# Two attentions in one kernel: maxima turned by one transpose a group, last values beside the spread, Q, K and V biases on ScalarE, the causal diagonal masked on VectorE behind the exponential

## The chip, the cores and the metric

The kernel runs on one core of a Trainium2 chip. The metric is the device time of one execution in microseconds (us). The engines are TensorE (PE in the rows, its weight loads PEld), VectorE (DVE), ScalarE (ACT), GpSimd (POOL) and SyncE (SP), which issues most DMAs.

## The reference

A layer of a gated cross-attention model on x of shape 8 x 512 x 512 (batch, tokens, channels), all in float32, cut to what matters:

```python
# pass A: cross attention, 16 heads of 32
Q = (layernorm(x) @ Wq + bq), K = (ctx @ Wk + bk), V = (ctx @ Wv + bv)   # split in heads
scores = Q @ K.T / sqrt(32) + rel_bias[:, clip(i - j, -63, 63) + 63]; masked keys -> -inf
x = x + tanh(g_xattn) * (softmax(scores) @ V @ Wo + bo)
# pass B: causal self attention with a latent K/V and rotary parts, 16 heads of 64
h = rmsnorm(layernorm(x), w_ln1)
q = h @ Wq, kv = (h @ Wkva)[..., :64] @ Wkvb, k_rope = (h @ Wkva)[..., 64:]
q = [q_nope, rope(q_rope)], k = [kv, rope(k_rope)], v = [kv, 0]
att = q @ k.T / sqrt(64); att = where(lower triangle, att, -inf)
y = layernorm(x) + softmax(att) @ v @ Wo
# pass C: router over 8 experts, top 2, and a shared expert; out = x + tanh(g_ffn) * (...)
```

## The kernel before

There are three passes, one behind the other: A (the cross attention, `pass_a`), B (the causal attention, `pass_b`), C (the experts, `pass_c`). The names of their tiles begin with a_, b_ and c_.

**Splits.** Products are made in float16 with a high and a low half of each operand (hi x hi, hi x lo, lo x hi, three matmuls in a row), so a tile that leaves PSUM is evicted twice: ScalarE copies it to the high half, then VectorE takes the low half as PSUM less high half.

**Steps.** Both attentions run over batches b of 64 steps, and each engine's program is written out by hand for the same 64 steps. Four heads are a group, and a group is 16 units (unit = head and key block of 128), one unit a step. At step s TensorE issues, in this order: the scores of unit s - 6, keys on partitions (L747 in pass A; L1504, L1505, L1506 in pass B); the product for the row maxima of the group after, queries on partitions (L760; L1521 and L1522); pieces of projections that stand in `plan` for this step (`fill`: Q, K, V and O, transposes of inputs, M and SP, below); and, at every fourth step, the four value products of the units up to s - 8 (L774; L1535), each on its own 32 columns of the array. Behind them, ScalarE takes the exponential of unit s - 6 (L497; L1258); in pass A VectorE adds the relative bias ahead of it (L604); VectorE reduces the maxima (L615; L1384), which leaves the negative of the maximum of 128 queries in one column of `low`; and GpSimd adds the exponentials of a head's key blocks into `acc`, for the softmax's sum (L407; L1169). PSUM banks for scores and for maxima are double: TensorE's scores of step s wait for the exponential of two units before, and its maxima for VectorE's reduction two steps before. The engines execute in order, so what waits holds all behind it.

**Maxima (job M of a group, steps 0, 16, 32, 48).** Four transposes turn `low`, 4 columns each, to 4 rows of 512 (L711; L1469); ScalarE copies them (L479; L1210) and a DMA on its queue lays them as one row into `q_stack`, so that the scores come out less their maximum.

**Spread (job SP, steps 8, 24, 40, 56).** Four float32 products with ones, again on 32 columns each, sum `acc` over partitions (L702; L1464). VectorE transposes, inverts, transposes back (L564 to L568; L1348 to L1352). ScalarE moves the values' bank to `o_un` (L523; L1287), GpSimd multiplies (L425; L1184), ScalarE makes the high half (L528; L1292), GpSimd the low half (L428; L1187), and the output projection O waits for it.

**Biases in pass A.** Each of Q, K, V and O ends with one more matmul, of ones and a row of the bias (L695). The bias rows are made at the start (L534, L535, L624). Each batch has four groups, so four jobs each of Q and K, and four each of V and O.

**Causal mask in pass B.** Only key blocks up to the diagonal are computed: of a unit with key block j the queries from 128 j on, so w = 512 - 128 j columns. The first 128 columns are the diagonal block; L1505 adds to them the product of two constants, `far` (1e15 times identity) and `hidden` (-1e15 above the diagonal), inside the chain of the scores.

## Time and profile before

| what | value |
|---|---|
| runs | 2417.91, 2419.53, 2424.08 us; median 2419.53 |
| profiled execution | 2419.89 us, of which the span from first to last instruction is 2418.0 |
| pass A | up to about 920 us |
| pass B | about 920 to 1830 us, with its loads |
| pass C | the rest |
| instructions | 50305, of which 12864 matmuls |

The profile is of one execution. Times in it are from the span's start. Matmuls overlap: a row's length is from its start to its modelled end, and the next may start long before. Two engines' rows are compared by their starts and ends. In a group's row the busy time is the union of its instructions, the mean that of one; behind the bar stands the engine's idle time just before them, and who ended it.

### The profile page before, as it was taken

To read this page: it belongs to the slowest core of one execution; us is meant where nothing else is said; L and a number is where in the kernel's file an instruction comes from. 1 tells how busy PE (TensorE), PEld (TensorE's weight loads), DVE (VectorE), ACT (ScalarE), POOL (GpSimd) and SP (SyncE) were. 2 spreads that over 40 slices of the span, in tenths; PEclk is the share of its full clock that TensorE was granted. 3 is DMA by queue.
4 is the path that set the end of the run, shared out by engine and by line. 5 is a ranking of instruction groups with operands and counts; after the bars stand their busy time and mean duration, and the time that the engine had idled before them with its cause. 6 is when DMAs were issued, how large, how long until landed. Compare 5 with 4: busy or idle time off the path is not lost. (4 is left out here: it accounts for less than half of the span.)

```text
span 2418.0 us, 50305 instructions
## 1 busy us (share of the span) xinstructions
PE 2171.5 (90%) x12864; PEld 982.9 (41%) x12865; DVE 1514.7 (63%) x4218; ACT 1197.2 (50%) x2316; POOL 1365.2 (56%) x1452
## 2 busy tenths in 40 slices
PE   3899999999999963899999999999985797899997
PEld 1333333333333311344444444444432343455554
DVE  3788888887888843556565565555533678344443
ACT  3355555554555442355545454454544574455554
POOL 3267677677677670264655564565561565455554
PEclk7999999999999986899999999999997899899999
DMA  5413323232232203543434353352414576666665
GB/s 173 147 57 107 97 86 110 70 110 87 96 106 75 80 9 129 146 118 117 147 94 135 101 154 117 101 156 88 134 50 136 86 178 132 106 114 114 111 109 91
DMA packets 221402, 264.60 MB, mean 109 GB/s; under 512 B 37400, under 2 KB 163468, under 8 KB 220852
## 3 DMA queue, kind: packets, MB, share of 16 engines
q1 hardware_dynamic: 197612, 212.79, 29.2%
q0 software_dynamic: 22976, 48.38, 11.6%
q8 instruction: 106, 1.74, 0.3%
q14 instruction: 172, 1.41, 0.2%
q10 hardware_dynamic: 536, 0.28, 0.0%
HBM read 162.12 MB, written 86.80 MB: 103 GB/s over the span
## 5 line engine op out<-in xcount | busy, mean ns | idle before, releaser
L497 ACT ACTIVATE a_pt<-a_bank 128x512 f32<-128x512 f32 x512 | 305.1, 597 | 356.2 <-DVE a_bank L604 343.5
L1384 DVE CUSTOM_DVE_ANT_0 b_bank<-b_bank,b_tri 128x256 f32<-128x256 f32 (+3 forms) x512 | 253.7, 497 | 322.7 <-PE b_bank L1522 320.3
L615 DVE CUSTOM_DVE_ANT_0 a_bank<-a_bank,a_strip 128x512 f32<-128x512 f32 x512 | 354.2, 693 | 7.3 <-PE a_bank L760 4.6
L1169 POOL TENSOR_TENSOR b_acc<-b_acc,b_pt 128x256 f32<-128x256 f32 (+2 forms) x384 | 271.7, 725 | 104.6 <-ACT b_pt L1258 88.0
L407 POOL TENSOR_TENSOR a_acc<-a_acc,a_pt 128x512 f32<-128x512 f32 x256 | 317.8, 1270 | 14.6 <-ACT a_pt L497 11.3
L604 DVE TENSOR_TENSOR a_bank<-a_bank,a_band 128x256 f32<-128x256 f32 (+1 forms) x512 | 205.6, 402 | 132.0 <-PE a_bank L747 130.2
L1258 ACT ACTIVATE b_pt<-b_bank 128x256 f32<-128x256 f32 (+2 forms) x384 | 143.4, 381 | 202.1 <-PE b_bank L1506 199.0
L747 PE MATMUL a_bank<-a_q_stack,a_k_stack 128*128 128x512 f16 x512 | 197.7, 388 | 14.6 <-ACT a_pt L497 10.2
L760 PE MATMUL a_bank<-a_k_stack,a_q_stack 97*128 97x512 f16 x512 | 196.3, 384 | 3.6 <-DVE a_low L615 3.5
L1850 POOL DMA_INDIRECT out_dram<-c_z,c_to_row x72 | 114.1, 1585 | 139.6 <-DMA out_dram<-c_z,c_to_row 106.5
L1504 PE MATMUL b_bank<-b_q_stack,b_k_stack 96*128 96x256 f16 (+3 forms) x512 | 155.5, 304 | 9.5 <-ACT b_pt L1258 6.4
L404 POOL TENSOR_TENSOR a_acc<-a_pt 128x512 f32<-128x512 f32 x128 | 160.0, 1271 | 4.3 <-ACT a_pt L497 4.3
L1521 PE MATMUL b_bank<-b_k_stack,b_q_stack 96*128 96x256 f16 (+3 forms) x512 | 154.6, 302 | 5.3 <-DMA b_q_stack<-qk_rows 3.0
L425 POOL TENSOR_TENSOR a_o_un<-a_o_un,a_den 128x512 f32<-128x512 f32 x32 | 40.8, 1276 | 202.7 <-DVE a_den L568 202.7
L1184 POOL TENSOR_TENSOR b_o_un<-b_o_un,b_den 128x512 f32<-128x512 f32 x32 | 40.7, 1273 | 201.5 <-DVE b_den L1352 195.6
L1506 PE MATMUL b_bank<-b_q_stack,b_k_stack 97*128 97x256 f16 (+3 forms) x512 | 153.3, 300 | 0.0
L1522 PE MATMUL b_bank<-b_k_stack,b_q_stack 96*128 96x256 f16 (+3 forms) x512 | 153.2, 300 | 0.0
L774 PE MATMUL a_bank<-a_pt,a_v 128*32 128x512 f32 x1024 | 138.1, 612 | 1.4 <-ACT a_pt L497 1.4
L747 PEld LDWEIGHTS a_bank<-a_q_stack,a_k_stack 128*128 128x128 f16 x512 | 49.4, 97 | 186.6 <-ACT a_pt L497 116.9
L1258 ACT ACTIVATE b_acc<-b_bank 128x512 f32<-128x512 f32 x128 | 76.5, 597 | 94.4 <-PE b_bank L1506 94.3
L1505 PE MATMUL b_bank<-b_hidden,b_far 128*128 128x128 bf16 x512 | 112.7, 220 | 0.0
L2230 DVE TENSOR_TENSOR c_xt_lo<-c_bank,c_xt_hi 128x512 f16<-128x512 f32 x72 | 49.8, 691 | 99.8 <-ACT c_xt_hi L1969 98.6
(346 smaller groups left out, 5501.8 us busy)
## 6 DMA issues: line engine op xcount, KB each, us to landing
b_q_stack<-qk_rows SPq DMA_DIRECT2D x192, 128.0 KB, 2.7
a_q_stack<-qk_rows SPq DMA_DIRECT2D x96, 128.0 KB
a_k_stack<-qk_rows SPq DMA_DIRECT2D x96, 128.0 KB
b_k_stack<-qk_rows SPq DMA_DIRECT2D x96, 128.0 KB, 2.6
a_sums<-in_x SPq DMA_DIRECT2D x34, 256.0 KB, 3.2
qk_rows<-a_qk_hi SPq DMA_DIRECT2D x64, 128.0 KB, 1.7
qk_rows<-a_qk_lo SPq DMA_DIRECT2D x64, 128.0 KB, 1.8
out_dram<-a_sums SPq DMA_DIRECT2D x32, 256.0 KB, 2.0
```

The costliest lines, as they stand in the source:

```text
L404: nc.gpsimd.tensor_tensor(acc[:, hh, :], pt[:, (n - HG) % SLOTS, :], mine, ALU.add).then_inc(pooled, 1)
L407: nc.gpsimd.tensor_tensor(acc[:, hh, :], acc[:, hh, :], mine, ALU.add).then_inc(pooled, 1)
L497: nc.scalar.activation(pt[:, n % SLOTS, :], st_bank[n % 2][:], ACT.Exp).then_inc(exped, 1)
L604: nc.vector.tensor_tensor(st_bank[n % 2][:, c0:c1], st_bank[n % 2][:, c0:c1], band[:, h, at:at + c1 - c0], ALU.add).then_inc(biased, 1)
L615: nc.vector.tensor_tensor_reduce(out=max_bank[step % 2][:], in0=max_bank[step % 2][:], in1=strip[:, g * HG + hh, at:at + S], scale=-1.0, s ...
L747: mm(st_bank[n % 2][:], k_stack[:, h, j * P:(j + 1) * P], q_stack[:, h, :], start=True, stop=True).then_inc(scored, 1)
L760: mm(max_bank[step % 2][:], q_stack[0:MASK + 1, h, i * P:(i + 1) * P], k_stack[0:MASK + 1, h, :], start=True, stop=True).then_inc(maxed, 1)
L1169: nc.gpsimd.tensor_tensor(sums_of, sums_of, probs(n), ALU.add).then_inc(pooled, 1)
L1258: nc.scalar.activation(probs(n), st_bank[n % 2][:, 0:w], ACT.Exp).then_inc(exped, 1)
L1384: nc.vector.tensor_tensor_reduce(out=max_bank[step % 2][:, 0:w], in0=max_bank[step % 2][:, 0:w], in1=tri[:, at:at + w], scale=-1.0, scalar ...
L1504: mm(o, k_stack[0][0:LOW, h, j * P:(j + 1) * P], q_stack[0][0:LOW, h, j * P:], start=True, stop=False)
L1521: mm(o, q_stack[0][0:LOW, h, c], k_stack[0][0:LOW, h, 0:w], start=True, stop=False)
```

## The change

- Pass A and B, M: `low` is laid out head by head (column hh x 4 + i), and one transpose of all 16 columns gives 16 rows of 128; ScalarE copies 16 x 128, and the DMA reads 16 rows.
- Pass A and B, SP: the last value products of a group (key block 3) move from step 7 to step 8 (of 16) and stand just ahead of the spread, which is now issued last in its step. ScalarE moves the bank at the ninth step, not the eighth.
- Pass A, biases: Q's and K's bias is added by ScalarE, as it evicts PSUM to a float32 tile `qk_row`; a second activation, which waits for the first, makes the high half from it, and VectorE makes the low half as `qk_row` less high half, from SBUF alone. V's bias is added to the normalized output, by one more activation on `o_un`. O's stays a matmul. The bias tile shrinks to one row of 512, and a tile `b_col` with the biases as columns is loaded by a DMA of its own.
- Pass B, mask: L1505 and its constants go. Behind the exponential VectorE takes, for each unit, the minimum of the diagonal 128 x 128 block and a constant `seen` (0 where masked, 3e38 elsewhere), in place. GpSimd's sum and the value products wait for that instead of for the exponential.

```diff
@@ pass_a, scalar @@
-                    nc.scalar.activation(qk_hi[:, 2 * (n % 2) + part, :], src, ACT.Copy, scale=(q_scale if m == Q else 1.0 / WS)
-                                         ).then_inc(hi_done, 1)
+                    if kind == "first" and n == 0:
+                        act.wait_ge(b_scaled, 1)
+                    if n == G3:
+                        act.wait_ge(left_dve, before(kind, b, by_dve))
+                    elif n or kind != "first":
+                        act.wait_ge(left_dve, upto(kind, b, (m, (n - 1) % NG), by_dve))
+                    nc.scalar.activation(qk_row[:, part, :], src, ACT.Identity, scale=(q_scale if m == Q else 1.0 / WS),
+                                         bias=b_col[:, part, n:n + 1]).then_inc(left_act, 1)
+                    act.wait_ge(left_act, upto(kind, b, job, by_act))
+                    nc.scalar.activation(qk_hi[:, 2 * (n % 2) + part, :], qk_row[:, part, :], ACT.Copy).then_inc(hi_done, 1)
...
-                    nc.scalar.activation(m_row[:, n % 2, :], src[0:HG, :], ACT.Copy).then_inc(left_act, 1)
+                    nc.scalar.activation(m_row[:, n % 2, :], src[0:NT * HG, 0:P], ACT.Copy).then_inc(left_act, 1)
...
-                        if off == 8:
-                            act.wait_ge(summed, b * (UNITS // HG) + (step - 8) // HG)
+                        if off == 9:
+                            act.wait_ge(summed, b * (UNITS // HG) + (step - 9) // HG)
...
+                            nc.scalar.activation(o_un[:], o_un[:], ACT.Identity, bias=b_col[:, 2, g:g + 1]).then_inc(v_biased, 1)
+                            act.wait_ge(v_biased, groups + 1)
                             nc.scalar.activation(o_hi[:, g, :], o_un[:], ACT.Copy).then_inc(o_hi_done, 1)
@@ pass_a, vector @@
+                    nc.vector.tensor_tensor(qk_lo[:, slot, :], qk_row[:, int(m == K), :], qk_hi[:, slot, :], ALU.subtract
+                                            ).then_inc(left_dve, 1)
+                    return
@@ pass_a, tensor @@
                 for i, (lhs, rhs) in enumerate(pairs):
-                    mm(o, lhs, rhs, start=(k == 0 and i == 0), stop=False)
+                    last = mm(o, lhs, rhs, start=(k == 0 and i == 0), stop=(k == NK - 1 and i == 2 and m != O))
                 if k == NK - 1:
-                    mm(o, *both, start=False, stop=True).then_inc(job_done, 1)
+                    if m == O:
+                        last = mm(o, ones[:], bias[:], start=False, stop=True)
+                    last.then_inc(job_done, 1)
...
-                for i in range(NT):
-                    last = nc.tensor.transpose(bank_of(kind, job)[0:HG, i * P:(i + 1) * P], low[:, g % 2, i * HG:(i + 1) * HG], idn[:])
-                last.then_inc(job_done, 1)
+                nc.tensor.transpose(bank_of(kind, job)[0:NT * HG, 0:P], low[:, g % 2, :], idn[:]).then_inc(job_done, 1)
...
@@ pass_b, vector @@
             def body(kind, b, u):
                 for step in range(STEPS):
+                    n = step - L - 1
+                    if has_unit(kind, n):
+                        dve.wait_ge(exped, b * UNITS + n + 1)
+                        nc.vector.tensor_tensor(probs(n)[:, 0:P], probs(n)[:, 0:P], seen[:], ALU.min).then_inc(masked, 1)
@@ pass_b, gpsimd @@
-                        pool.wait_ge(exped, b * UNITS + n + 1)
+                        pool.wait_ge(masked, b * UNITS + n + 1)
@@ pass_b, tensor @@
                         mm(o, k_stack[0][0:LOW, h, j * P:(j + 1) * P], q_stack[0][0:LOW, h, j * P:], start=True, stop=False)
-                        mm(o[:, 0:P], far[:], hidden[:], start=False, stop=False)
...
-                    fill(kind, b, step)
-                    n = step - L - 2
-                    if has_unit(kind, n) and n % HG == HG - 1:
+                    fill(kind, b, step, False)
+                    beside = (step - L - 2) % GS == 0
+                    n = step - L - 2 - beside
+                    if has_unit(kind, n) and n % HG == HG - 1 and (beside or n % GS != GS - 1):
...
-                        pe.wait_ge(exped, b * UNITS + n + 1)
+                        pe.wait_ge(masked, b * UNITS + n + 1)
...
+                    fill(kind, b, step, True)
```

How the rows move, at three places. On TensorE in pass B, from a group's last value products to its spread (steps 23 and 24, SP of group 0; L1535 are the values, L1464 is the spread), before:

```order
L1535 MATMUL b_bank<-b_pt,b_v 32x128 x4
L1504 MATMUL b_bank<-b_q_stack,b_k_stack 128x512
L1505 MATMUL b_bank<-b_hidden,b_far 128x128
L1506 MATMUL b_bank<-b_q_stack,b_k_stack 128x512
L1518 REGISTER_ALU
L1521 MATMUL b_bank<-b_k_stack,b_q_stack 128x256
L1522 MATMUL b_bank<-b_k_stack,b_q_stack 128x256
L1417 REGISTER_ALU
L1462 REGISTER_ALU
L1464 MATMUL b_bank<-b_acc,b_ones_f 32x512 x4
```

and in the changed kernel, where L1552 are the values and L1482 is the spread:

```order
L1443 MATMUL b_bank<-b_wo_hi,b_o_hi 128x512
L1444 MATMUL b_bank<-b_wo_lo,b_o_hi 128x512
L1445 MATMUL b_bank<-b_wo_hi,b_o_lo 128x512
L1521 MATMUL b_bank<-b_q_stack,b_k_stack 128x512
L1522 MATMUL b_bank<-b_q_stack,b_k_stack 128x512
L1534 REGISTER_ALU
L1537 MATMUL b_bank<-b_k_stack,b_q_stack 128x256
L1538 MATMUL b_bank<-b_k_stack,b_q_stack 128x256
L1552 MATMUL b_bank<-b_pt,b_v 32x128 x4
L1435 REGISTER_ALU
L1480 REGISTER_ALU
L1482 MATMUL b_bank<-b_acc,b_ones_f 32x512 x4
```

The values have moved behind the scores and maxima of the next step, next to the spread, and the masking product L1505 is gone. On VectorE in pass B, from the end of the first spread's inversion to the split of the rotary query (steps 41 to 44; L1384 are maxima, `b_rc` and `b_qu_lo` the split), before:

```order
L1352 STREAM_TRANSPOSE b_den<-b_rden 128x512
L1382 REGISTER_ALU
L1384 ISA b_bank,b_low<-b_bank,b_tri 128x256
L1384 ISA b_low 128x1
L1382 REGISTER_ALU
L1384 ISA b_bank,b_low<-b_bank,b_tri 128x256
L1384 ISA b_low 128x1
L1316 REGISTER_ALU
L1323 TENSOR_TENSOR b_rc<-b_bank,b_rot 128x512
L1335 SCALAR_TENSOR_TENSOR b_qu_lo<-b_bank,b_qu_hi 128x512
L1382 REGISTER_ALU
L1384 ISA b_bank,b_low<-b_bank,b_tri 128x128
```

and in the changed kernel, where L1394 is the mask and L1402 are the maxima:

```order
L1366 STREAM_TRANSPOSE b_den<-b_rden 128x512
L1394 TENSOR_TENSOR b_acc<-b_acc,b_seen 128x128
L1400 REGISTER_ALU
L1402 ISA b_bank,b_low<-b_bank,b_tri 128x256
L1402 ISA b_low 128x1
L1394 TENSOR_TENSOR b_pt<-b_pt,b_seen 128x128
L1400 REGISTER_ALU
L1402 ISA b_bank,b_low<-b_bank,b_tri 128x256
L1402 ISA b_low 128x1
L1330 REGISTER_ALU
L1337 TENSOR_TENSOR b_rc<-b_bank,b_rot 128x512
L1349 SCALAR_TENSOR_TENSOR b_qu_lo<-b_bank,b_qu_hi 128x512
```

A mask stands ahead of each maximum. On ScalarE in pass A, around an eviction of K and the copy of the maxima (L497 are exponentials), before:

```order
L497 ACTIVATE a_pt<-a_bank 128x512 x3
L471 ACTIVATE a_qk_hi<-a_bank 128x512
L497 ACTIVATE a_pt<-a_bank 128x512
L479 ACTIVATE a_m_row<-a_bank 4x512
L497 ACTIVATE a_pt<-a_bank 128x512
L501 DMA a_q_stack<-a_m_row 1x4x512
```

and in the changed kernel, where L508 are exponentials:

```order
L508 ACTIVATE a_pt<-a_bank 128x512 x3
L480 ACTIVATE a_qk_row<-a_bank,a_b_col 128x512
L483 ACTIVATE a_qk_hi<-a_qk_row 128x512
L508 ACTIVATE a_pt<-a_bank 128x512
L490 ACTIVATE a_m_row<-a_bank 16x128
L508 ACTIVATE a_pt<-a_bank 128x512
L512 DMA a_q_stack<-a_m_row 1x16x128
```

The eviction has become two activations, one behind the other, and the copy of the maxima is 16 x 128.

## Rows read from the trace of the kernel before

**Rows 1.** Busy time of stages of pass A and of pass B.

```profile
100.00:800.00 700.00, 685.99 (x3693) 263.12 (x3694) 587.97 (x1592) 389.27 (x690) 497.70 (x463) 1.00 0.29 92
1010.00:1800.00 790.00, 763.61 (x5323) 373.10 (x5324) 462.42 (x1360) 393.06 (x837) 441.83 (x575) 1.00 0.40 118
```

**Rows 2.** Order of time on TensorE, pass A: start, length, line, tiles.

```profile
453.26 0.38 PE L693 MATMUL a_bank<-a_w_hi,a_ct_lo 128*128 128x512 f16 x1
453.47 0.38 PE L695 MATMUL a_bank<-a_bias,a_ones 128*128 128x512 f16 x1
453.78 1.06 PE L774 MATMUL a_bank<-a_pt,a_v 128*32 128x512 f32 x8
```

**Rows 3.** Order of time on TensorE, pass B.

```profile
1400.30 0.22 PE L1505 MATMUL b_bank<-b_hidden,b_far 128*128 128x128 bf16 x1
1400.36 0.22 PE L1506 MATMUL b_bank<-b_q_stack,b_k_stack 97*128 97x128 f16 x1
```

**Rows 4.** Groups by shape on TensorE, whole run; last row: 1400 to 1500 us alone.

```profile
L1505 PE MATMUL b_bank<-b_hidden,b_far 128*128 128x128 bf16 x512 | 112.7, 220 | 0.0
...
L695 PE MATMUL a_bank<-a_bias,a_ones 128*128 128x512 f16 x64 | 24.7, 386 | 0.0
...
L1505 PE MATMUL b_bank<-b_hidden,b_far 128*128 128x128 bf16 x63 | 13.9, 220 | 0.0
```

**Rows 5.** Order of time on TensorE, pass B, steps 32 and 33.

```profile
1370.26 0.60 PE L1469 MATMUL b_bank<-b_idn,b_low 128*4 128x128 f32 x4
1370.69 0.27 PE L1504 MATMUL b_bank<-b_q_stack,b_k_stack 96*128 96x256 f16 x1
...
1371.19 0.38 PE L1522 MATMUL b_bank<-b_k_stack,b_q_stack 96*128 96x512 f16 x1
1372.52 0.39 PE L1425 MATMUL b_bank<-b_ht_hi,b_wq_hi 128*128 128x512 f16 x1 [0.95 <-DVE b_qu_lo L1335]
```

**Rows 6.** Order of time on ScalarE, start of the run.

```profile
9.11 1.91 ACT L535 ACTIVATE a_bias<-a_v 1x2048 f16<-1x2048 f32 x1
```

**Rows 7.** Order of time, pass A, K of group 3: ScalarE, then VectorE.

```profile
402.69 0.58 ACT L471 ACTIVATE a_qk_hi<-a_bank 128x512 f16<-128x512 f32 x1
...
403.37 0.69 DVE L579 SCALAR_TENSOR_TENSOR a_qk_lo<-a_bank,a_qk_hi 128x512 f16<-128x512 f32 x1
404.58 0.37 DVE L604 TENSOR_TENSOR a_bank<-a_bank,a_band 128x192 f32<-128x192 f32 x1 [0.52 <-PE a_bank L747]
```

**Rows 8.** Busy time of 11.9 us in pass A, of 8 us in pass B.

```profile
404.60:416.50 11.90, 11.83 (x66) 4.92 (x64) 10.81 (x29) 7.05 (x13) 8.78 (x8) 1.00 0.49 157
...
1420.90:1428.90 8.00, 8.00 (x60) 3.78 (x64) 7.35 (x21) 3.29 (x7) 2.98 (x7) 1.00 0.26 84
```

**Rows 9.** Groups by shape on VectorE, whole run.

```profile
L1384 DVE CUSTOM_DVE_ANT_0 b_bank<-b_bank,b_tri 128x128 f32<-128x128 f32 x128 | 38.3, 299 | 75.2 <-PE b_bank L1522 74.0
```

**Rows 10.** Order of time, pass C: GpSimd, then VectorE, twice.

```profile
1891.83 1.16 POOL L1770 TENSOR_TENSOR c_h_lo<-c_hid,c_h_hi 128x512 f16<-128x512 f32 x1 [5.21 <-ACT c_h_hi L1919]
...
1892.20 1.34 DVE L2014 SCALAR_TENSOR_TENSOR c_gu_lo<-c_gu_stage,c_wn,c_gu_hi 128x512 f16<-128x512 f32 x1
...
1893.46 0.74 DVE L2014 SCALAR_TENSOR_TENSOR c_gu_lo<-c_gu_stage,c_wn,c_gu_hi 128x512 f16<-128x512 f32 x1
```

**Rows 11.** Order of time, pass B, steps 42 to 46: VectorE, GpSimd, TensorE.

```profile
1387.36 0.40 DVE L1384 CUSTOM_DVE_ANT_0 b_bank<-b_bank,b_tri 128x256 f32<-128x256 f32 x1
...
1389.68 0.14 DVE L1384 DVE_READ_ACCUMULATOR2_ANT b_low<- 128x1 f32 x1
...
1387.52 1.28 POOL L1184 TENSOR_TENSOR b_o_un<-b_o_un,b_den 128x512 f32<-128x512 f32 x1 [5.29 <-DVE b_den L1352]
1388.82 2.90 POOL L1169 TENSOR_TENSOR b_acc<-b_acc,b_pt 128x384 f32<-128x384 f32 x3
...
1390.15 0.22 PE L1521 MATMUL b_bank<-b_k_stack,b_q_stack 96*128 96x128 f16 x1
```

**Rows 12.** Order of time on TensorE, pass B, step 15.

```profile
1337.83 0.39 PE L1425 MATMUL b_bank<-b_wo_hi,b_o_hi 128*128 128x512 f16 x1 [0.70 <-POOL b_o_lo L1187]
```

More of the change, by code:

```diff
@@ L216, in by_dve @@
         def by_dve(j):
-            return j[0] not in on_act
+            return j[0] not in (V, M)
         def ended(kind, step):
@@ L678, in product @@
                     pairs = ((w_hi[:, w, k, c], h[:, k, :]), (w_hi[:, w, k, c], l[:, k, :]), (w_lo[:, w, k, c], h[:, k, :]))
-                    both = (bias[:, w, c], ones[:].unsqueeze(1).broadcast_to([P, NT, P]))
                     if k == 0 and n < G3:
@@ L685, in product @@
                     pairs = ((h[:, k, c], w_hi[:, w, k, :]), (h[:, k, c], w_lo[:, w, k, :]), (l[:, k, c], w_hi[:, w, k, :]))
-                    both = (ones[:], bias[:, w, :])
                     if m == O:
@@ L1467, in job_piece @@
                     pe.wait_ge(lowered, b * UNITS + (n + 1) * GS)
-                    for i in range(NT):
-                        last = nc.tensor.transpose(o[0:HG, i * P:(i + 1) * P], low[:, n % 2, i * HG:(i + 1) * HG], idn[:])
+                    last = nc.tensor.transpose(o[0:NT * HG, 0:P], low[:, n % 2, :], idn[:])
                 else:
@@ L2447 @@
     for name in ("x", "ctx_1024", "mask_BxS2_bf0", "g_xattn", "g_ffn") + tuple(
-            "L0_xattn_" + n for n in ("Wq", "bq", "Wk", "bk", "Wv", "bv", "Wo", "bo")):
+            "L0_xattn_" + n for n in ("Wq", "Wk", "Wv", "Wo", "bo")):
         give(name, inputs[name])
+    give("bias_columns", _np.stack([_np.asarray(inputs["L0_xattn_" + n]).reshape(NG, P).T for n in ("bq", "bk", "bv")], 1))
     rel = _np.asarray(inputs["L0_xattn_rel_bias"])
@@ L2496 @@
     give("causal", _np.where(_np.arange(STRIP)[None, :] - (NT - 1) * P <= _np.arange(P)[:, None], 0, -1e30).astype(_np.float32))
-    give("later", _np.where(_np.arange(P)[:, None] > _np.arange(P)[None, :], -1e30, 0).astype(_np.float32))
+    give("later", _np.where(_np.arange(P)[:, None] > _np.arange(P)[None, :], 0, 3e38).astype(_np.float32))
     out = nc.dram_tensor("out_0_dram", (B, S, D), F32, kind="ExternalOutput").ap()
```

70 lines of the change are left out of this document (36 added, 34 removed).

## The prediction

> **What bounds the kernel now.** I read the busy time by stage first. In a stretch inside pass A TensorE is busy for 686.0 of 700 us, in one inside pass B for 763.6 of 790 us; VectorE has 84% and 59% there, ScalarE 56% and 50%, GpSimd 71% and 56% [rows 1]. A busy TensorE can hide gaps, since each matmul's end is modelled and overlaps the next one's start, so I went on to the order of time. The starts are packed: 0.215 us from one 512-column product to the next [rows 2], 0.06 us from one of 128 columns to the next [rows 3]. So both attentions run at TensorE's pace, and matmuls taken out there can shorten them. In pass A VectorE is close behind; in pass B it has room on the average, not at each place. Pass C and the loads between the passes are not touched.
>
> **What TensorE no longer does.**
> (a) Bias products of pass A. Q and K have 64 [rows 4], V and O 32 each (four a batch). O's stay, so 96 go. One takes 0.215 us, the step from the last product to the bias product [rows 2]: 96 x 0.215 = 20.6 us.
> (b) The masking product of pass B, 512 of them [rows 4], 0.06 us from start to start [rows 3]: 30.7 us. Its mean of 220 ns is latency and not the price.
> (c) Maxima. Four transposes take 1370.26 to 1370.69, 0.43 us, so 0.107 each [rows 5]. Three of four go: 0.32 us x 32 groups = 10.3 us in each pass. The one left has the same 128 columns, and four times the weight columns, which hide as others do.
> (d) Last values beside the spread. Before a group on 32-column tiles 0.31 us pass instead of 0.215 [rows 2]; the 0.09 us is paid at each change of tiling. Two such groups now adjoin, so one entry goes: 0.09 x 32 = 2.9 us in each pass.
> Gross: pass A 20.6 + 10.3 + 2.9 = 33.8 us, pass B 30.7 + 10.3 + 2.9 = 43.9 us; per batch 4.2 and 5.5.
> (e) Before the first product, two copies of bias rows stand on ScalarE ahead of the first normalization, 1.91 us each for 2048 elements [rows 6]. With 512 elements each takes what a 512-element activation takes, 0.59 [rows 7]; 2 x 1.32 = 2.6 us earlier, if x and Wq are there by then. I take it whole; nothing is the other end.
>
> **What pass A gives back.** ScalarE evicts Q and K in two dependent steps, 0.59 [rows 7] and 0.6, so the high half is ready some 0.65 us later. VectorE's low half then waits for it, and now reads two SBUF tensors. At the end of K of group 3 no room is left: the high half ends at 403.27, the low half starts at 403.37 [rows 7], so it starts 0.65 later, and the 0.52 us of idle behind it covers most. From there VectorE is busy for 10.81 of 11.90 us [rows 8], so it sets the pace there, and what TensorE saves at that place (two Q/K biases, one V bias, one entry, 0.74 us) comes back as waits. With the 0.13 not covered: 0.9 us a batch. At the evictions of groups 0 to 2 the bounds are nothing (VectorE is not late for TensorE's second step after) and the 0.65 plus a wait behind GpSimd (below: an operation's length less 0.19; 497.7 / 463 = 1.07 us on average here [rows 1]), 1.5 us at each of the two or three places without idle time; I choose 0.8 a batch in all, nearer the lower end, since most low halves start over 1 us after their high half. Sum 1.7 x 7 batches = 12 us; between 5 (the returned 0.74 alone) and 22. V's added step on ScalarE (0.6 us a group) lies behind GpSimd's backlog, the shorter copy of the maxima (16x128 for 4x512) relieves ScalarE, and the bank of Q and K comes free one step earlier. Net of pass A: **-22** (-12 to -29).
>
> **What pass B gives back.** No row shows the new operation on 128x128 SBUF elements. The nearest is the same width out of PSUM, 299 ns [rows 9]; below it nothing excludes 0.2, above 0.4; I take 0.30. 512 of them are 154 us of VectorE, 0.30 us a step of 1.6 us (63 masking products in 100 us [rows 4]). VectorE has 0.59 x 1.6 = 0.94 us a step now, and would have 1.24 of 1.5. It stands in front of the step's maximum, and behind it wait GpSimd's sum, the value products, and TensorE's maxima two steps later. Where VectorE idles it costs nothing.
> It has a second price. A VectorE instruction with two SBUF inputs took 1.34 us where it started 0.37 us into a GpSimd tensor operation of 1.16 us, and 0.74 us a moment later, alone [rows 10]: it stood still until GpSimd was done, 0.60 us. In the attentions' steady part no VectorE instruction had two SBUF inputs; now each mask has. GpSimd is busy 56% of pass B with operations of 0.77 us on average (441.8 / 575) [rows 1]; a mask at random meets one with 0.56 and waits about half a length less 0.19, so 0.1 to 0.2 us in the mean. I take 0.15: VectorE at 1.39 of 1.5 us.
> The Trainium skill says of the same ("SBUF — State Buffer", section "Who interferes with whom") that VectorE with two SBUF inputs and a GpSimd instruction that reads SBUF lock each other out for a whole instruction. By that, GpSimd also stands still behind each mask, and VectorE behind each sum; a price of 0.30 without it would make the mask free nearly everywhere.
> Places: (1) Behind the first spread the split of the rotary query (QR) keeps VectorE without idle from 1387.36; the maximum is read out at 1389.82, and TensorE takes its bank at 1390.15, 0.33 us to spare [rows 11]. Three masks stand in that stretch: 0.90 - 0.33 = 0.6 us late; GpSimd is busy all through it, so up to 2.1. I take 1.3. (2) In steps 3 to 8 VectorE is busy 7.35 of 8.00 us [rows 8]; five masks need 1.5, 0.65 is free, and the lead of two steps covers 0.85, but not with locks: 0 to 1.9, I take 0.8. (3) TensorE waits for the QR split already, 0.95 us after the product of 1371.19 [rows 5]; the 0.38 us saved just ahead (c and one b) only lengthens that. (4) It waits 0.70 us for O's low half from GpSimd [rows 12]; the 0.5 us saved since the spread comes back, and the chain spread, VectorE, GpSimd, ScalarE, GpSimd grows by a mask or two: 0.8 to 1.4, I take 1.1. Other banks freed by VectorE: 0.3.
> Sum 1.3 + 0.8 + 0.4 + 1.1 + 0.3 = 3.9 x 7 = 27 us (12 to 43). Net of pass B: **-17** (-32 to -1).
>
> **Sum.** -22 - 17 - 2.6 = -41.6 us. From the execution's 2419.9 (span 2418.0 and 1.9 around it), which is 0.4 above the median 2419.5: 2378.
>
> **Rivals.**
> R1, the masks eat pass B's gain, no more: VectorE's stalls are those of the upper ends, 3.9 becomes 6.1. Then only pass A and the start give: 2419.5 - 24.6 = 2395. For it: the locks, GpSimd's unbroken 2.90 us [rows 11]. Against it: GpSimd's sum of a unit starts at its mask, so it is mostly over by the next.
> R2, slower: VectorE becomes pass B's bound. Its load is 0.94 + 0.30 + lock; it passes the old step of 1.6 us from a lock of 0.36 us a mask on, and outweighs pass A (25 us / 512 = 0.05) from 0.41 on. At 0.5 it gives 512 x 0.14 = 72 us more for pass B, 2419.5 - 24.6 + 72 = 2467. That needs nearly every mask behind a GpSimd operation; the 56% speaks against it. (The lock that the Trainium skill describes on the page named above is its mechanism.)
> R3, cheap: the leads of two steps cover the masks, and only returned savings are lost (0.74 x 7 in pass A, 0.4 + 0.5 + 0.3 a batch in pass B): 2419.5 - 29 - 36 - 2.6 = 2352.
> R4, nothing moves, because the row pipelines around TensorE (ScalarE's exponentials in the order scores, bias, exponential) were the real pace: against it stand the packed starts. Only the start's 2.6 us are left: 2417.
>
> **Chances.** Forecast (2365 to 2388) 0.60; R1 0.16; R3 0.13; R2 0.06; R4 0.05. The range reaches from R3 to above R1: 2350 to 2404. A change of 0.3% (7 us) is what a measurement of this kernel tells from none: faster 0.88, same 0.06, slower 0.06.
>
> **What the profile would show.** (b) and (c): the masking product gone, one transpose of 16 columns a group; 12864 TensorE instructions less 512, 96 and 192. Pass A shorter by some 22 us, pass B by some 17. Step (d): the group of values and the spread 0.1 us closer. Masks at 0.30 us with a tail to 1 us; the low half of Q and K with a tail above 0.69. TensorE's longest new waits for VectorE's maxima behind the first spread, and longer ones for the QR split and for O's low half. The prediction is wrong if masks average over 0.6 us, or if TensorE's waits on VectorE in pass B stay as they are now.

## The result and the profile after

The changed kernel takes 2435.4 us (median of 5 executions, 2428.1 to 2441.9) against 2420.1 before: ratio 1.0059, 95% interval 1.0033 to 1.0084. It is slower by 15 us, where a time 42 us shorter was forecast. Its profiled execution took 2438.6 us, span 2435.9.

The page of the changed kernel, its totals and the granted clock in 40 slices:

```profile
span 2435.9 us, 49533 instructions
PE 2124.2 (87%) x12064; PEld 934.9 (38%) x12065; DVE 1733.0 (71%) x4731; ACT 1236.9 (51%) x2410; POOL 1399.9 (57%) x1452
PEclk7999999999999976899999999999986898899999
```

The edits show in the counts: 12864 less 12064 is 800 TensorE instructions, the 512 + 96 + 192 of the forecast. So the work is gone and the time is not. Below is the busy time of the stretches of [rows 1] in the changed kernel (columns: TensorE, weight loads, VectorE, ScalarE, GpSimd, granted clock, DMA share, GB/s), then that of all of pass B and of two of its batches:

```profile
100.00:800.00 700.00, 657.70 (x3506) 249.61 (x3507) 601.38 (x1586) 427.63 (x767) 511.26 (x462) 1.00 0.29 91
1010.00:1800.00 790.00, 732.68 (x4679) 339.29 (x4677) 643.24 (x1841) 380.77 (x823) 446.92 (x562) 0.98 0.41 120
1014.40:1848.50 834.10, 763.06 (x4847) 348.37 (x4847) 669.45 (x1884) 394.36 (x857) 470.33 (x591) 0.97 0.38 114
1110.00:1212.10 102.10, 96.24 (x628) 45.14 (x627) 86.03 (x244) 50.97 (x111) 60.34 (x77) 1.00 0.43 125
1526.50:1634.10 107.60, 101.70 (x629) 46.76 (x627) 85.17 (x241) 50.88 (x109) 57.24 (x74) 0.95 0.43 127
```

TensorE has 42 us of idle time in the first stretch (14 before) and 57 in the second (26 before), VectorE went from 59% to 81% in the second, and the clock is no longer at its full level all through it. Two batches of one kernel with the same instructions take 102.1 us at clock 1.00 and 107.6 at 0.95. So I split the time three ways, in every run: **a clean batch** (the shortest of batches 1 to 6 of 0 to 7, from a batch's first maximum product to the next one's; no fall of the clock is in it), **the loop's edge** (the body holds two batches; where it is entered again TensorE idles 2.00 and 2.26 us in pass B before), and **the half clock** (the time between pass B's batch 0 and pass C for which the clock records show 1.2 GHz and not 2.4).

By the starts of instructions the span of the changed kernel differs from that of before so: up to pass A's batch 0 +0.6 us, six batches of pass A +4.9 (614.3 for 609.4), from there to pass B nothing, pass B +11.9 (834.2 for 822.3), pass C +0.6. Forecast were -2.6 for the start, about -19 for the six batches and -17 for pass B. Of pass B's 11.9 us its first six batches hold 4.0, and what lies behind them, to the start of pass C, 7.9 (214.5 for 206.6).

Groups by shape, changed kernel (busy, mean ns, idle before); the last row is that of before:

```profile
L1394 DVE TENSOR_TENSOR b_pt<-b_pt,b_seen 128x128 f32<-128x128 f32 x384 | 228.9, 599 | 27.9 <-ACT b_pt L1275 25.2 <-issue 2.3
L1394 DVE TENSOR_TENSOR b_acc<-b_acc,b_seen 128x128 f32<-128x128 f32 x128 | 40.0, 313 | 2.6 <-ACT b_acc L1275 2.6
L591 DVE TENSOR_TENSOR a_qk_lo<-a_qk_row,a_qk_hi 128x512 f16<-128x512 f32 x64 | 70.3, 1098 | 32.4 <-ACT a_qk_hi L483 31.8
L480 ACT ACTIVATE a_qk_row<-a_bank,a_b_col 128x512 f32<-128x512 f32 x64 | 43.7, 683 | 21.5 <-PE a_bank L707 21.5
L539 ACT ACTIVATE a_o_un<-a_o_un,a_b_col 128x512 f32<-128x512 f32 x32 | 22.9, 715 | 6.4 <-POOL a_o_un L428 6.4
L763 PE MATMUL a_bank<-a_q_stack,a_k_stack 128*128 128x512 f16 x512 | 199.3, 392 | 37.3 <-ACT a_pt L508 31.5 <-issue 5.0
...
L747 PE MATMUL a_bank<-a_q_stack,a_k_stack 128*128 128x512 f16 x512 | 197.7, 388 | 14.6 <-ACT a_pt L497 10.2 <-issue 4.0
```

The masks average 0.525 us (268.9 / 512), where 0.45 was forecast. The low half of Q and K takes 1.10 us for the 0.69 of [rows 7], and TensorE's scores wait 31.5 us for exponentials where they waited 10.2 before.

Order of time, changed kernel, pass B behind the first spread, the place of [rows 11]: VectorE, GpSimd, TensorE.

```profile
1392.06 1.07 DVE L1394 TENSOR_TENSOR b_pt<-b_pt,b_seen 128x128 f32<-128x128 f32 x1
1394.59 0.28 DVE L1394 TENSOR_TENSOR b_pt<-b_pt,b_seen 128x128 f32<-128x128 f32 x1
...
1391.70 1.28 POOL L1201 TENSOR_TENSOR b_o_un<-b_o_un,b_den 128x512 f32<-128x512 f32 x1 [4.87 <-DVE b_den L1366]
1393.29 1.00 POOL L1186 TENSOR_TENSOR b_acc<-b_acc,b_pt 128x384 f32<-128x384 f32 x1 [0.31 <-DVE b_pt L1394]
1394.95 0.99 POOL L1186 TENSOR_TENSOR b_acc<-b_acc,b_pt 128x384 f32<-128x384 f32 x1 [0.66 <-DVE b_pt L1394]
...
1395.19 0.23 PE L1537 MATMUL b_bank<-b_k_stack,b_q_stack 96*128 96x128 f16 x1 [0.71 <-DVE b_low L1402]
1397.36 0.85 PE L1552 MATMUL b_bank<-b_pt,b_v 128*32 128x384 f32 x8 [0.67 <-DVE b_pt L1394]
```

The mask at 1392.06 finds GpSimd busy until 1392.98 and ends 0.15 us behind it; the one at 1394.59 finds it idle and takes 0.28. TensorE then waits 0.71 us for a maximum, as forecast, and 0.67 us for a mask in front of the values, which no term of the forecast held.

### The profile page after: what moved, and what is told of

Same layout as the page of the kernel before. It is cut to its first block and busy times, and to the rows that moved or that the text cites. A ratio compares the mean times of both kernels' runs of the same rounds, so it can differ in the third digit from the quotient of the medians.

```text
span 2435.9 us, 49533 instructions
## 1 busy us (share of the span) xinstructions
PE 2124.2 (87%) x12064; PEld 934.9 (38%) x12065; DVE 1733.0 (71%) x4731; ACT 1236.9 (51%) x2410; POOL 1399.9 (57%) x1452
## 5 line engine op out<-in xcount | busy, mean ns | idle before, releaser
L508 ACT ACTIVATE a_pt<-a_bank 128x512 f32<-128x512 f32 x512 | 304.2, 596 | 328.2 <-DVE a_bank L619 321.8
L1186 POOL TENSOR_TENSOR b_acc<-b_acc,b_pt 128x256 f32<-128x256 f32 (+2 forms) x384 | 281.2, 740 | 163.1 <-DVE b_pt L1394 149.8
L1402 DVE CUSTOM_DVE_ANT_0 b_bank<-b_bank,b_tri 128x256 f32<-128x256 f32 (+3 forms) x512 | 252.7, 494 | 122.0 <-PE b_bank L1538 119.4
L410 POOL TENSOR_TENSOR a_acc<-a_acc,a_pt 128x512 f32<-128x512 f32 x256 | 327.1, 1306 | 9.6 <-ACT a_pt L508 5.6
L1394 DVE TENSOR_TENSOR b_pt<-b_pt,b_seen 128x128 f32<-128x128 f32 x384 | 228.9, 599 | 27.9 <-ACT b_pt L1275 25.2
L763 PE MATMUL a_bank<-a_q_stack,a_k_stack 128*128 128x512 f16 x512 | 199.3, 392 | 37.3 <-ACT a_pt L508 31.5
L407 POOL TENSOR_TENSOR a_acc<-a_pt 128x512 f32<-128x512 f32 x128 | 166.2, 1316 | 4.2 <-ACT a_pt L508 4.2
```

What stands on the lines that cost most here:

```text
L407: nc.gpsimd.tensor_tensor(acc[:, hh, :], pt[:, (n - HG) % SLOTS, :], mine, ALU.add).then_inc(pooled, 1)
L410: nc.gpsimd.tensor_tensor(acc[:, hh, :], acc[:, hh, :], mine, ALU.add).then_inc(pooled, 1)
L508: nc.scalar.activation(pt[:, n % SLOTS, :], st_bank[n % 2][:], ACT.Exp).then_inc(exped, 1)
L763: mm(st_bank[n % 2][:], k_stack[:, h, j * P:(j + 1) * P], q_stack[:, h, :], start=True, stop=True).then_inc(scored, 1)
L1186: nc.gpsimd.tensor_tensor(sums_of, sums_of, probs(n), ALU.add).then_inc(pooled, 1)
L1394: nc.vector.tensor_tensor(probs(n)[:, 0:P], probs(n)[:, 0:P], seen[:], ALU.min).then_inc(masked, 1)
```

## The experiments

Each ratio is to the kernel before on the same chip, 95% intervals in brackets. Times in us. The half clock counts from pass B's first batch to pass C; the edges are TensorE's idle times at the two places in pass B where the loop is entered again. Batches and clock are each read from one profiled execution.

| kernel | ratio | clean batch A | clean batch B | edges B | half clock B |
|---|---|---|---|---|---|
| before | 1 | 101.2 | 103.3 | 2.0, 2.3 | 6.8 |
| changed | 1.0059 [1.0033, 1.0084] | 101.6 | 102.1 | 3.0, 3.1 | 47.8 |
| e1 maxima and values | 0.9923 [0.9909, 0.9938] | 101.2 | 101.5 | 2.7, 1.9 | 3.4 |
| e2 biases | 1.0064 [1.0051, 1.0078] | 102.0 | 103.3 | 3.2, 3.4 | 17.0 |
| e3 masks | 1.0116 [1.0099, 1.0134] | 101.2 | 103.9 | 5.5, 4.4 | 47.8 |
| e4 all but masks | 0.9974 [0.9965, 0.9984] | 101.6 | 101.5 | 2.1, 1.9 | 3.4 |
| e5 values in pass B only | 0.9899 [0.9883, 0.9915] | 99.9 | 101.5 | 2.0, 2.6 | 0 |
| e6 Q and K biases | 1.0059 [1.0043, 1.0074] | 101.7 | 103.3 | 3.6, 3.8 | 27.3 |
| e7 low half from PSUM | 1.0040 [1.0024, 1.0056] | 101.2 | 103.3 | 3.7, 1.8 | 17.0 |
| e8 masks, one input | 1.0066 [1.0051, 1.0082] | 101.2 | 103.1 | 5.4, 5.8 | 37.5 |
| e9 masks on scores | 0.9963 [0.9951, 0.9975] | 101.2 | 101.6 | 3.1, 2.7 | 23.9 |
| e10 e5 less K's bias | 0.9900 [0.9882, 0.9917] | 99.0 | 101.5 | 2.1, 2.2 | 0 |
| e11 e10 and e9 | 0.9891 [0.9876, 0.9906] | 99.0 | 100.2 | 2.6, 2.6 | 13.7 |
| e12 masks added | 1.0159 [1.0144, 1.0174] | 101.2 | 106.5 | 5.2, 4.7 | 41.0 |

Unchanged code is not of the same length in every kernel. Pass A is untouched in e3, e8, e9 and e12, and its clean batch is 101.2 us in all of them as before, but its six batches took 609.3 to 616.2 us against 609.4, with batch 0 at 97.6 to 102.3 us against 96.0. Pass B is untouched in e2, e6 and e7 and took 5.6, 12.0 and 5.7 us more than before. So the clean batches tell more than the whole times, and a difference of 7 us in six batches of pass A tells nothing by itself.

### The change in its parts: e1 to e4

Before plus single transposes and moved values (e1), plus the biases (e2), plus the masks (e3); the changed kernel with the product `far` x `hidden` back and no mask (e4).

> The kernel before with only the two edits that take time from TensorE and give it to nobody: one transpose a group for the maxima, and the last values beside the spread, in both passes. TensorE loses 10.3 + 2.9 = 13.2 us in each pass. Theory T (the loss of the whole change sits in the two parts that put work on ScalarE and VectorE, namely the biases and the masks): most of the 26.4 us shows, ratio 0.990 to 0.994, some 2400 us. Rival P (pass A is at the pace of its row pipeline, VectorE being busy 84% there, so whatever TensorE saves in pass A comes back as waits): only pass B's half shows, ratio 0.995 to 0.997, and pass A from the first step of batch 0 to that of batch 6 stays at 609 us. Rival Q (the values moved one step later hold up the sums and the normalization behind them): ratio 1.000 or above.

> The kernel before with only the biases of Q, K and V moved to ScalarE. TensorE loses 96 bias products, 20.6 us. Theory T: the added step of 0.68 us before the high half, the added 0.72 us behind the normalization, and a low half that takes 1.10 us for 0.69 us delay VectorE's addition in front of the exponentials; pass A gets longer, not shorter. The whole change left pass A 5 us longer where 33.8 us of TensorE's work were gone. If the maxima and values give their 13 us in pass A, the biases alone cost 10 to 20 us, ratio 1.004 to 1.008. Rival P (pass A has another pace than TensorE's, and none of the edits matters much there): ratio 0.999 to 1.002.

> The kernel before with only the masks moved to VectorE. TensorE loses 512 masking products, 30.7 us. Theory T: the masks average 0.50 to 0.55 us (0.525 in the changed kernel), and pass B gets 5 to 25 us longer, ratio 1.002 to 1.010. Rival R (the masks are fine by themselves and only together with the moved values and the shorter steps do they miss their place): ratio 0.990 to 0.997, and TensorE's waits for VectorE's maxima behind the first spread are absent.

> The changed kernel with the masking product back on TensorE and no mask on VectorE. If the four parts add up, this is the sum of the first two runs of this call. Theory T: pass B gives its 13 us, pass A stays where the changed kernel has it (5 us longer than before), so ratio 0.995 to 0.999. Rival P: the same for pass B, and pass A within 2 us of the run that has the biases alone.

Theory T's range holds for e1, e2 and e4; e3 came out its way and above its range (1.0116, where 1.010 was the end). The maxima and values give 0.8%, the biases cost 0.6% alone (in its profiled execution 9 of 22 us lie in passes B and C, which it leaves alone) and the masks 1.2%. The product of e1 and e2 is 0.9987, e4 measured 0.9974; the masks on top of e4 cost 0.85% (1.0059 / 0.9974) where they cost 1.16% alone, so the parts add up to within 0.3%. But e1 gave rival P something: pass A took 607.6 us for six batches, 1.8 us less where 9.9 were expected, and its clean batch stayed at 101.2. Order of time on TensorE, before (L774 values, L702 spread, L693 V's first product), then e1 (L773, L702, L693):

```profile
400.97 1.06 PE L774 MATMUL a_bank<-a_pt,a_v 128*32 128x512 f32 x8
...
402.50 1.06 PE L702 MATMUL a_bank<-a_acc,a_ones_f 128*32 128x512 f32 x8
403.50 0.39 PE L693 MATMUL a_bank<-a_w_hi,a_ct_hi 128*128 128x512 f16 x1
```

```profile
398.56 0.38 PE L758 MATMUL a_bank<-a_k_stack,a_q_stack 97*128 97x512 f16 x1
400.11 0.39 PE L693 MATMUL a_bank<-a_w_hi,a_ct_hi 128*128 128x512 f16 x1 [1.17 <-DVE a_qk_lo L579]
...
400.86 1.06 PE L773 MATMUL a_bank<-a_pt,a_v 128*32 128x512 f32 x8
401.74 1.04 PE L702 MATMUL a_bank<-a_acc,a_ones_f 128*32 128x512 f32 x8
```

Before, values and spread, 2 us of TensorE, stand ahead of the product that needs the bank of K's or Q's last low half. The edit put both behind it, and TensorE meets the wait with nothing queued ahead of it.

### Pass A: the values' place (e5), the biases' parts (e6, e7)

```diff
 (e5: pass_a, tensor, back to)
+                    fill(kind, b, step)
+                    n = step - L - 2
+                    if has_unit(kind, n) and n % HG == HG - 1:
```

> The first run of the study (single transposes and last values beside the spread in both passes) with the values of pass A put back where they were before, so that pass A has only the single transposes. In that first run pass A from the first step of batch 0 to that of batch 6 took 607.6 us against 609.4 before: of 9.9 us expected for six batches 1.8 came. Its trace has new waits of TensorE there, 1.25 us in step 8 of each batch for VectorE's low half of K (10.0 us in eight batches) and 0.97 us in step 24 for the low half of the context (5.8 us in six). Theory C (the last values were the cover of these waits: moved behind step 8's and 24's jobs they leave TensorE idle first): both waits are gone, pass A takes 599 to 603 us for the six batches, ratio 0.988 to 0.991. Rival P (pass A is at the pace of VectorE's row pipeline): 606 to 609 us, ratio as in the first run, 0.992.

Theory C holds: 599.3 us for six batches, a clean batch 1.3 us shorter than in e1, and 1.3 shorter than before, which is the single transposes' 4 x 0.32. The wait in step 8 is gone in seven batches of eight, the one in step 24 in all. In pass B, transposes and moved values together gave 1.8 us a batch (101.5 for 103.3), where (c) and (d) come to 1.7.

```diff
 (e6: only Q and K on ScalarE)
-                            nc.scalar.activation(o_un[:], o_un[:], ACT.Identity, bias=b_col[:, 2, g:g + 1]).then_inc(v_biased, 1)
+                    if m in (O, V):
+                        last = mm(o, ones[:], bias[:, int(m == O), :], start=False, stop=True)
 (e7: e2 with the low half from PSUM)
-                    nc.vector.tensor_tensor(qk_lo[:, slot, :], qk_row[:, int(m == K), :], qk_hi[:, slot, :], ALU.subtract ...
+                    nc.vector.scalar_tensor_tensor(out=qk_lo[:, slot, :], in0=src, scalar=..., in1=qk_hi[:, slot, :], ...
```

> The run with the biases alone, with V's bias back in its product, so that only Q and K have theirs on ScalarE. That run was 1.0064 of before, pass A 618.2 us for six batches against 609.4. Theory V (V's step of 0.72 us on ScalarE, which stands between two exponentials at step 12 of each group, is the larger part: TensorE waits for the exponentials in steps 46 and 30): ratio 0.998 to 1.001. Rival L (the low half of Q and K with its two SBUF inputs, 1.04 to 1.10 us for 0.69, and the later high half are the larger part): ratio 1.003 to 1.006. The low half's mean stays at 1.0 to 1.1 us either way.

> The run with the biases alone, with the low half of Q and K computed from PSUM and the high half as before, one SBUF input instead of two. ScalarE's two steps stay. The biases of Q and K are left out of the result by it, since the low half cancels what the high half holds of them. The bank comes free one VectorE instruction later, as before the change. Theory L (VectorE with two SBUF inputs waits for GpSimd and holds it up): the low half's mean falls from 1.1 to 0.69 us, GpSimd's sums in pass A from 1.31 to 1.27 us, and pass A gets 5 to 9 us shorter, ratio 0.999 to 1.003. Rival S (ScalarE's longer chain is what costs): the low half falls to 0.69 all the same, but ratio 1.004 to 1.007.

e6's ratio is rival L's, though 6 us of it are pass B's, which is untouched and longer than in e2. Its clean batch is 0.3 us shorter than e2's with 0.9 us of TensorE's work put back, so V's step costs 1.2 us a batch and saves 0.9. In e7 the low half is at its old length and GpSimd's sums too (1.272 us; 1.307 in e2), as expected, and a clean batch is 0.8 us shorter. Six batches are 3.6 us shorter where Theory L wanted 5 to 9, and the ratio 1.0040 stands at the lower end of rival S's range. Groups by shape on VectorE, e7:

```profile
L591 DVE SCALAR_TENSOR_TENSOR a_qk_lo<-a_bank,a_qk_hi 128x512 f16<-128x512 f32 x64 | 44.0, 688 | 33.3 <-ACT a_qk_hi L483 33.2
```

So of the biases' price in a clean batch (2.6 us saved and 0.8 longer, 3.4) the second SBUF input is 0.8, by e7. The other 2.6 are not taken apart by a run. TensorE's idle time for exponentials shows part of them: none in a clean batch before, 2.4 us in six places in the changed kernel. In three (0.95 us) the exponential stands behind ScalarE's own added steps; in the other three (1.43 us) ScalarE itself waits for VectorE's addition of the relative bias. Where ScalarE's steps bite, order of time in the changed kernel, step 45 to 46 of pass A: ScalarE, then TensorE.

```profile
466.57 0.58 ACT L508 ACTIVATE a_pt<-a_bank 128x512 f32<-128x512 f32 x1
467.05 0.71 ACT L539 ACTIVATE a_o_un<-a_o_un,a_b_col 128x512 f32<-128x512 f32 x1
467.79 0.63 ACT L541 ACTIVATE a_o_hi<-a_o_un 128x512 f16<-128x512 f32 x1
468.33 0.58 ACT L508 ACTIVATE a_pt<-a_bank 128x512 f32<-128x512 f32 x1
...
468.97 0.39 PE L763 MATMUL a_bank<-a_q_stack,a_k_stack 128*128 128x512 f16 x1 [0.50 <-ACT a_pt L508]
```

V's added step and the high half fill the whole time between two exponentials, and TensorE's next scores wait for the bank of the second.

### Pass B: the masks' price, place and cover (e8, e9, e12)

```diff
 (e8: e3 with)
+                        nc.vector.tensor_scalar(probs(n)[:, 0:P], probs(n)[:, 0:P], 3e38, None, ALU.min).then_inc(masked, 1)
 (e9: before less the masking product, and the exponential waits for masked)
+                    n = step - L
+                    if has_unit(kind, n):
+                        dve.wait_ge(scored, b * UNITS + n + 1)
+                        nc.vector.tensor_tensor(st_bank[n % 2][:, 0:P], st_bank[n % 2][:, 0:P], seen[:], ALU.add).then_inc(masked, 1)
 (e12: before, the masking product kept, e3's waits, and)
+                        nc.vector.tensor_tensor(probs(n)[:, 0:P], probs(n)[:, 0:P], tri[:, 0:P], ALU.max).then_inc(masked, 1)
```

> The run with the masks alone, with each mask replaced by a minimum with a constant: the same place, size and waits, but one SBUF input instead of two. It masks nothing, so the causal mask is left out of the probabilities. The run with masks had 0.60 us for 384 and 0.31 us for 128 of them, ratio 1.0116. Theory L (half of the price is the wait for GpSimd, which comes with the second SBUF input): the mean falls to 0.2 to 0.3 us for both groups, GpSimd's sums from 0.737 to 0.726 us, ratio 0.993 to 1.001. Rival D (the price is the place: one more instruction and one more hand-over in front of each maximum and each sum): the ratio stays above 1.006.

e8 came out by rival D's ratio, but it did not take the wait for GpSimd away, so it does not separate the two. Groups by shape on VectorE, e8:

```profile
L1376 DVE TENSOR_SCALAR b_pt<-b_pt 128x128 f32<-128x128 f32 x384 | 202.7, 530 | 21.3 <-ACT b_pt L1257 12.7 <-issue 7.5
L1376 DVE TENSOR_SCALAR b_acc<-b_acc 128x128 f32<-128x128 f32 x128 | 32.3, 253 | 2.6 <-ACT b_acc L1257 2.6
```

With GpSimd idle it took 0.22 us (0.28 with two inputs), but 268 of 512 started inside a GpSimd instruction, and these averaged 0.68 us. The Trainium skill ("SBUF — State Buffer", section "Who interferes with whom") says this: `tensor_scalar` from SBUF to SBUF can run in a mode that takes both ports, and then shares GpSimd's lock as an instruction with two inputs does. The trace agrees. GpSimd's sums, though, were back at 0.727 us (0.737 in e3, 0.725 before), and the ratio fell by 0.5%.

> The kernel before with the masking product of pass B taken from TensorE, as in the run with the masks alone, but VectorE masks the scores in PSUM ahead of the exponential (an addition of a 128x128 tile) and not the exponentials in SBUF behind it. One SBUF input, so no wait for GpSimd; the same 512 instructions; GpSimd and the values wait for the exponential alone, as before the change. The nearest row is pass A's addition of 128x192, 0.37 us; 128 columns should take 0.29 to 0.30. Theory L (the wait for GpSimd and the hand-over behind the exponential are what the masks cost): ratio 0.988 to 0.997, TensorE at the half clock in pass B for under 10 us, pass B's clean batches 101.5 to 102.5 us against 103.3. Rival D (one more instruction on VectorE in each step is too much in any place): ratio 1.000 to 1.007.

Theory L's ratio and its clean batch hold; its half clock of under 10 us does not (10.2 in six batches, 23.9 in all). Groups by shape on VectorE, e9, then the busy time of e9's stretch in pass B:

```profile
L1376 DVE TENSOR_TENSOR b_bank<-b_bank,b_seen 128x128 f32<-128x128 f32 x512 | 152.0, 298 | 162.0 <-PE b_bank L1505 159.1
...
1010.00:1800.00 790.00, 750.84 (x4852) 345.25 (x4850) 579.16 (x1870) 400.01 (x843) 444.81 (x576) 0.99 0.41 119
```

With the same width, the same number, one operand in PSUM and a place ahead of the exponential, a mask takes 298 ns, which is the row I had for the price [rows 9]. The kernel is 37 us shorter than e3's by the ratios (0.0153 x 2420). So the product can be taken from TensorE at a gain. e9 differs from e3 in the place, the operand and who waits for the mask, all at once, and no run tells their shares apart.

> The kernel before with the masks added on VectorE in SBUF behind the exponential and the masking product left on TensorE, so that TensorE saves nothing (the mask takes the larger of the exponential and a tile of zeros and large negative numbers, which changes nothing). The run with the masks alone had clean batches of 103.9 us in pass B against 103.3 before, where 3.8 us of TensorE's work were gone: 4.4 us of waits a batch. Theory B (VectorE's row sets pass B's pace then, and the waits are TensorE's time come back): the waits shrink by the 3.8 us put back, clean batches 103.9 to 104.5 us, the clock falls less often, ratio 1.004 to 1.012. Rival A (each place is late by itself, whatever TensorE does between them): clean batches near 107.7 us, ratio 1.020 to 1.030.

Neither theory: with TensorE's product kept a clean batch takes 106.5 us, 3.2 over before, where e3's waits were 4.4 (103.9 less 103.3, and 3.8 saved). Read so, 3.2 us of the masks' waits a batch are lateness at their places, whatever TensorE saves, and 1.2 are its saved time coming back.

The edge and the clock, e3: TensorE in order of time over the loop's edge, and the busy time of a clean batch and the one behind it.

```profile
1314.40 0.85 PE L1534 MATMUL b_bank<-b_pt,b_v 128*32 128x384 f32 x8 [0.46 <-DVE b_pt L1376]
1320.74 0.39 PE L1504 MATMUL b_bank<-b_q_stack,b_k_stack 96*128 96x256 f16 x1 [5.49 <-issue]
...
1321.13 0.63 PE L1520 MATMUL b_bank<-b_k_stack,b_q_stack 96*128 96x512 f16 x1
...
1106.70:1210.60 103.90, 98.51 (x640) 45.57 (x638) 86.78 (x244) 51.82 (x111) 60.20 (x77) 1.00 0.41 123
1210.60:1321.60 111.00, 100.49 (x640) 46.19 (x639) 88.59 (x247) 52.28 (x112) 63.74 (x81) 0.96 0.41 118
```

TensorE idles 5.49 us there, the granted clock falls to 0.5, and a product of 512 columns takes 0.63 us where it took 0.38. The batch is 7.1 us longer than the clean one ahead of it.

The edge is not the only place, nor the main one. In the changed kernel the clock falls nine times in pass B, and 10 of its 47.8 us at half are at the edges. Three falls (14 us) stand in steps 45 and 46 of batches 0, 5 and 6, behind the new waits for a maximum and for a mask; the last four (24 us) are in batch 7, behind waits of 0.6 to 1.7 us for masks and maxima and one of 2.05 for O's low half. Before, there are two falls of 3.4 us, at an edge and in batch 7. Changed kernel, order of time on TensorE in step 45 and behind it, then the busy time of what follows (clock 0.50):

```profile
1604.71 0.23 PE L1537 MATMUL b_bank<-b_k_stack,b_q_stack 96*128 96x128 f16 x1 [0.72 <-DVE b_low L1402]
...
1606.88 1.51 PE L1552 MATMUL b_bank<-b_pt,b_v 128*32 128x384 f32 x8 [0.67 <-DVE b_pt L1394]
...
1606.50:1613.00 6.50, 6.12 (x24) 2.36 (x25) 5.24 (x14) 1.72 (x5) 5.88 (x8) 0.50 0.81 220
```

The group of values takes 1.51 us there, and 0.85 in the same place of another batch (1397.36 above). Batches 1 to 4 have the same two waits and no fall there.

### What paid, together: e10 and e11

```diff
 (e10: e5, pass_a, tensor)
-                    mm(o, *both, start=False, stop=True).then_inc(job_done, 1)
+                    if m != K:
+                        last = mm(o, *both, start=False, stop=True)
+                    last.then_inc(job_done, 1)
```

> The best run so far (single transposes in both passes, last values beside the spread in pass B alone; 0.9899) with K's bias product left out and nothing put in its place: what it adds to a row of scores is the same for every key, so the softmax cancels it. 32 products of 0.215 us go, 6.9 us. Theory (TensorE sets pass A's pace where no other engine got work): a clean batch of pass A falls from 99.9 to 99.0 us, ratio 0.986 to 0.988. Rival P (pass A has reached the pace of its row pipeline, VectorE being at 85% and more): nothing comes, ratio 0.989 to 0.991.

> What paid, together: single transposes in both passes, last values beside the spread in pass B, K's bias product left out (this much was 0.9900), and the masks on the scores in PSUM (alone 0.9963). If the two add up: ratio 0.984 to 0.988, and a clean batch of pass B takes 99.6 to 100.2 us against 101.6 and 101.5 with the one and with the other. Rival D (the masks' gain is used up once TensorE has less to do, since VectorE then has 1.24 us of work in a step under 1.6 us): clean batches of pass B above 101 us, ratio 0.989 to 0.992.

e10's clean batch of pass A is the 99.0 us expected, but the ratio is that of e5: rival P's number with the theory's batches. By the trace the six batches gave 2.3 us where 5.1 were due, its first and sixth being 0.7 and 0.6 us longer than e5's, and pass C took 593.5 us where e5's took 587.6 with the same code. What 6.9 us do can't be told from whole times here. In e11 the clean batch of pass B is 100.2 us, 1.3 less than in e10 and at the end of what the sum of the two gave, but the half clock is 13.7 us against none, and the ratio 0.9891 is rival D's and not the 0.984 to 0.988 of the sum. It is the lowest of the study and can't be told from e5 and e10, whose intervals hold it. All three beat the kernel before by 1.0 to 1.1%.

## Why the prediction was wrong

**What bounded the kernel** was read rightly: matmuls taken out shorten both passes at TensorE's pace where nothing else is added (e5: 99.9 and 101.5 us; e10: 99.0). Rival R4 falls with that.

**(a) to (c)**, the gross terms, hold: 800 instructions went, the single transposes' 1.3 us a batch in pass A are shown alone by e5 against before, and four bias products give 0.9 by e10 against e5.

**(d) failed in pass A.** "Two such groups now adjoin, so one entry goes" priced the tiling and not what the move uncovers: e1 against e5, 1.3 us a batch lost, 0.36 saved, so 1.7 given up. I costed it at nothing without naming the work that the values hid, and 0.36 + 1.3 over eight batches are 13 us of the error by the clean batches (the ratios of e1 and e5 give the move some 6 us, within wide intervals).

**(e)** gave nothing: the first batch came 0.6 us later, not 2.6 earlier. Pass A's batch 0 starts at 85.1 to 88.1 us in the nine kernels with all the old bias rows, at 88.1 in e6 and at 88.7 to 89.5 in the four with one row. No run tries this edit alone, so why it is later stays open.

**Pass A's return** was sized at 1.7 us a batch and measured 4.7 (4.2 saved, and 0.5 longer). The values' place is one part. The other is ScalarE, for which the prediction had "V's added step ... lies behind GpSimd's backlog": it lies between two exponentials, and TensorE waits for the second (0.50 us in the row above). Of the 2.4 us a batch that TensorE newly idles for exponentials, ScalarE's own steps are 0.95, which the sum had at nothing, and VectorE's lateness is 1.43, for which it had 0.8 at the evictions. The low half's wait for GpSimd was in the bounds; its mean of 1.10 us is 0.8 us a batch by e7.

**Pass B's places** were nearly right in sum: a clean batch fell by 1.2 us and 5.5 were taken out, so 4.3 came back where I had 3.9. Place (3) took 0.38 more (1.33 us against the 0.95 of [rows 5]), as forecast; (4) 0.5 more (1.20 against the 0.70 of [rows 12]), half of the forecast; (1) about 1.2 in steps 45 and 46, as forecast; (2) at most 0.4, but for one wait of 1.23 us behind an edge. What came on top is the values' wait for their own masks: in the changed kernel TensorE comes to them 1.8 us a batch later than in e4, which has no mask, by the starts of its instructions. The prediction names it ("behind it wait GpSimd's sum, the value products") and prices only the maxima.

**The lock was mis-sized** (a mask's wait for GpSimd): 284 of 512 masks started inside a GpSimd instruction, 0.55, as forecast from 56%. But these took 0.73 us, 0.45 more than a mask alone, not the 0.2 more of "half a length less 0.19". The GpSimd instruction that they met was 1.00 us long on average, not 0.77, since a long one is met more often, and 0.42 us of it were over. "GpSimd's sum of a unit starts at its mask, so it is mostly over by the next" is so far right: 155 of 512 masks met a sum. The other 129 met GpSimd's other work, 1.12 us long on average, which this argument left out. A mask alone takes 0.28, not 0.30. By R2's own threshold (0.36 a mask) the lock's mean, 0.24, was short of making VectorE the bound, and a clean batch did get shorter: R2's sign came, its mechanism did not.

**The missing term is the clock, behind the new waits and at the edge.** A clean batch of pass B is 1.2 us shorter, and pass B is 11.9 longer: its first six batches are 4.0 us longer where six clean ones would be 7 shorter, and what lies behind them is 7.9 longer. The half clock, 47.8 us against 6.8, costs half of the difference where TensorE sets the pace: at most 20 us of pass B. No rival had this. The forecast priced each wait at its own length; where the clock falls behind it, it costs more (5.5 us between two batches of the same instructions above). Falls stand behind e3's edge and behind the waits for masks in steps 45 and 46, but not behind each such wait, so when one falls stays open. The longest edges are those of three kernels with the masks behind the exponential (e3, e8, e12: 4.4 to 5.8 us), but the changed kernel has 3.0 and 3.1, like e9, with the mask ahead of it (3.1 and 2.7). Why the edge grows stays open: e9 has as many instructions on VectorE as e3, and e2, e6 and e7, with pass B's code unchanged, have edges up to 3.8 us and 17 to 27 us of half clock. Their code for pass B is the same and lies elsewhere in the program, a rival that no run tested. No run changed the edge or the clock by itself, so their share is worked out from the records and not shown by an experiment.

So the steps that failed are (d) and ScalarE's added steps in pass A, each put at nothing, and in pass B the waits' price, without the values' wait, with too short a lock and without the clock. No rival had it: for pass B's clean batches the forecast's own 3.9 us are nearer than R1's 6.1, and R4's time, the nearest to the measured one, has another cause.

## What to carry to other kernels

Work moved on the bounding engine's queue is a change of cover: before moving it, list which wait stands behind it and what would stand ahead of that wait afterwards. In this kernel a mask on VectorE paid where its operand is in PSUM and ahead of the exponential, and not on SBUF behind it: a mask of the same size took 298 ns there and the kernel got 0.4% shorter (e9), and behind the exponential some 530 ns with the kernel 1.2% longer (e3). When an edit gives TensorE new waits, count the clock as a term of the sum, and compare a clean batch with the average one before explaining a difference.
